# Delta stage of a decoder kernel: values turned token-major as pairs of f16 products instead of f32 transposes

## The chip, the cores and the metric
One core of a Trainium2 chip. The metric is the device time of one execution in microseconds (us): the median of several runs. The engines are TensorE (PE, its weight loads PEld), VectorE (DVE), ScalarE (ACT), GpSimd (POOL) and SyncE (SP), each with an instruction queue of its own that it works in order; semaphores tie them together.

## The reference
Two decoder layers over 8 sequences of 256 tokens with 512 features, a layer norm after every block. The change touches one block, the second layer's attention, a gated delta rule with 16 key heads of 128 and two value heads for each:

```
mixed = silu(causal_conv4(x @ Wqkv.T))        # query, key: 16 x 128 channels; value: 32 x 128
query, key = l2norm(query), l2norm(key)
beta, g = sigmoid(b), -exp(A_log) * softplus(a + dt_bias)
for t:                                         # a state of 128 x 128 per head
    state = state * exp(g_t)
    delta = (v_t - k_t @ state) * beta_t
    state = state + outer(k_t, delta)
    out_t = q_t @ state
out = (rmsnorm(out) * norm_w * silu(x @ Wz.T)) @ Wout.T
```

## The kernel before
The whole decoder is one program of stages, one after the other. The delta stage (function `delta_stage`) takes two thirds of its time. It solves the recurrence in chunks of 128 tokens: for each chunk a triangular system is inverted in seven levels (`level_a`, `level_b` on TensorE, `level_p`, `level_xt` on VectorE, `level_x` on ScalarE), and the rest are matrix products.

The work is cut into 64 units: for each of the 16 key heads four units (`it.u` = 0 to 3) of 512 tokens, that is two sequences of two chunks, with both value heads. The stage is a software pipeline over units: `turns(turn)` calls on each engine the same function once a turn, and in turn n an engine works on parts of the units n+2 (projection, convolution, silu), n+1 (products of keys, inverse), n (answers) and n-1, n-2 (output). `it.has(off)` asks whether there is such a unit; `after(name, k, off)` waits until the k-th signal of that name of unit n+off has come. The order within a turn is written out by hand, at the end of each engine's `turn`, and an engine never leaves it. Work that comes once in four turns (splitting the next key head's weights into an f16 high part, on ScalarE, and a low part, on VectorE) is in the same lists: `next_qkv` when it.u(2) is 3, `next_turns_weights` a turn later, `next_z` another turn later, `next_o` when it.u(-1) is 0.

f32 values meet TensorE as pairs of f16: `high` is ScalarE's cast to f16 and `low` is GpSimd's subtraction, value minus high. So the keys and queries (`products_high`, L1909; `products_low`, L1704) and the decayed products (`split_high`, L1920; `split_low`, L1748).

The values (unit n+2, jobs v0 and v1, one value head each): TensorE's projection goes to a PSUM bank, ScalarE's `conv_tap` writes the first tap into `F[:, 2 + v]` (L1949) and the farthest one into `far[:, v]` (L1955), VectorE's `conv_lag` (L2145) adds two taps from the bank, GpSimd's `conv_far` (L1695) adds `far`, and ScalarE's `silu_job` (L1964) works in place in `F`. In the next turn TensorE's `values_token_major` turns the 8 blocks of 128x128 by f32 transposes (L2565), and ScalarE's `token_major` (L1933) takes them out of PSUM. `far` has two buffers, used by q and v0 and by k and v1.

ScalarE's list around the place of the change, and GpSimd's:

```python
silu_job("v0"); gate(0); products_high(0); products_high(1); split_high(0); split_high(1)
conv_tap("v1"); level_x(1, 1); next_qkv(0); next_qkv(1); split_high(2); split_high(3)
first_answer(1); gate(1); level_x(2, 1); silu_job("v1"); next_qkv(2)
sc.preload_act_table_set("natural_log_exp_and_others"); key_norm(); next_z(0); next_z(1)
decays(0, 2); level_x(3, 1); output_squares(0, 0)          # end of ScalarE's turn
# GpSimd: ... squares_low(1); products_low(0); products_low(1); gm sums; cju copy;
#   conv_far("v1"); split_low(0); V16; split_low(1); low_L(0); split_low(2); low_L(1); split_low(3)
```

`level_x` is L1893. On TensorE `level_a(4)` (L2482) opens the next turn and waits for the third `level_x`; VectorE splits the z weights (`low`, L2083) behind ScalarE's split (L1801), and its `add_out` (L2286) frees the bank that the next projection job takes.

Of the kernel before, what the change touches and what calls it, by code (L numbers as in the profile page):

```python
# [7 lines left out]
F16 = mybir.dt.float16  # L8
BF16 = mybir.dt.bfloat16
ALU = mybir.AluOpType  # L10
ACT = mybir.ActivationFunctionType
# [3 lines left out]
P = 128  # L15
# [1382 lines left out]
def delta_stage(nc, X, consts, WbaT, dtb, alog, Wqkv, Wz, Wout, convw, normw, gt_dram):  # L1398
    with ExitStack() as ctx:
        pt = Parts(nc, "delta", ctx)  # L1400
        sb, counter = pt.sb, pt.counter
        bank = pt.banks()
        ident, ident16 = consts["ident"], consts["ident16"]
# [22 lines left out]
        F = sb("F", [P, 4, 512])  # L1426
# [24 lines left out]
        g = {}  # L1451
        for name, per in dict(
            qj=4, zj=2, wj=4, tap0=4, taps=8, far=4, conv=4, silu=4, sq=2, zsilu=2, wadd=4,
            fh=2, fl=2, sql=2, kss=1, qss=1, ke=1, lnk=1, sk=1, rk2=1, eq=1, gm=4, cju=1, e=8,
            s=3, la=8, dg=2, lt=2, ll=2, vt=2, v=2, v16=1,
            pa=7, px=5, pd=6, pm=7, xc=5, xt=7, xir=1, xti=1,
            sv=7, u0=2, r=2, w=2, t16=1, t2=1, o=2,
            ahi=4, alo=4, so=8, rr=1, lr=1, rn0=1, rn=3, ogs=8, og=2, ct=2, ch=2, cl=2,
        ).items():
            g[name] = counter(name, per)  # L1460
# [51 lines left out]
        def high_half(i):  # L1512

            return sq[:, i, :].bitcast(BF16).rearrange("p (n h) -> p n h", h=2)[:, :, 1]

        def cw_tap(t, k):
            return cw[:, t * 4 + k:t * 4 + k + 1]
# [89 lines left out]
        def _(pool):  # L1607
# [57 lines left out]
            def turn(it):  # L1665
# [24 lines left out]
                def conv_far(job):  # L1690
                    i = QKV[job]
                    after("taps", 2 * i + 2, 2)
                    after("far", i + 1, 2)
                    dst, src = (t.rearrange("p (b t) -> p b t", b=2) for t in (F[:, i, :], far[:, i % 2, :]))
                    gp.tensor_tensor(dst[:, :, 3:256], dst[:, :, 3:256], src[:, :, 0:253], ALU.add)\  # L1695
                        .then_inc(g["conv"].sem, 1)
# [44 lines left out]
                def split_low(n):  # L1741
                    after("ahi", n + 1, 1)
                    if n != 2:
                        after("o", 2, -1)
                    else:
                        after("sv", 4, 0)
                    by_sequencer()
                    gp.tensor_tensor(split_to(n, it.u(1), 1), LA[:, :, split_from[n]:split_from[n] + P],  # L1748
                                     split_to(n, it.u(1), 0), ALU.subtract).then_inc(g["alo"].sem, 1)

                if it.has(2):
                    conv_far("v1")
                if it.has(1):
                    split_low(0)
# [23 lines left out]
                if it.has(1):  # L1778
                    low_L(1)
                    split_low(3)  # L1780

            turns(turn)

        @block.scalar
        def _(act):
# [41 lines left out]
            def turn(it):  # L1827
                def after(name, k, off):
                    if it.has(off):
                        act.wait_ge(g[name].sem, g[name].at(k, it.n(off)))  # L1830
# [72 lines left out]
                def products_high(i):  # L1903

                    if not it.has(2):
                        return
                    after("silu", i + 1, 2)
                    after("s", 3, 1)
                    sc.activation(Fh[:, :, 1 - i, :], by_half(i), ACT.Copy).then_inc(g["fh"].sem, 1)  # L1909
# [27 lines left out]
                def conv_tap(job):  # L1937

                    if not it.has(2):
                        return  # L1940
                    i = QKV[job]
                    after("qj", i + 1, 2)
                    if job == "q":
                        after("s", 3, 1)
                        if it.u(2) == 0:
                            act.wait_ge(w_c.sem, w_c.at(1, it.kh(2)))
                    if job == "v0":
                        after("vt", 2, 1)
                    sc.activation(F[:, i, :], bank[AT[job] % 2][:, :], ACT.Copy, scale=cw_tap(i, 3))\  # L1949
                        .then_inc(g["tap0"].sem, 1)  # L1950
                    if i < 2:
                        after("conv", 3 + i, 1)
                    else:
                        after("conv", i - 1, 2)
                    sc.activation(far[:, i % 2, :], bank[AT[job] % 2][:, :], ACT.Copy, scale=cw_tap(i, 0))\  # L1955
                        .then_inc(g["far"].sem, 1)

                def silu_job(job):

                    if not it.has(2):  # L1960
                        return
                    i = QKV[job]
                    after("conv", i + 1, 2)
                    sc.activation(F[:, i, :], F[:, i, :], ACT.Silu).then_inc(g["silu"].sem, 1)  # L1964
                    if i < 2:
                        after("silu", i + 1, 2)
                        after("kss", 1, 1)
                        after("qss", 1, 1)
                        sc.activation(sq[:, i, :], F[:, i, :], ACT.Square).then_inc(g["sq"].sem, 1)

                def gate(t):

                    if not it.has(0):
                        return
                    after("zj", 1 + t, 0)
                    after("og", 2, -1)
                    sc.activation(flat(gz[:, 2 * t:2 * t + 2, :]), bank[AT[f"z{t}"] % 2][:, :], ACT.Silu, scale=CS)\  # L1977
                        .then_inc(g["zsilu"].sem, 1)
# [10 lines left out]
                def next_qkv(c):  # L1989
                    if it.u(2) == 3 and it.has(2):  # L1990
                        after("qj", 1 + c, 2)
                        high("qkv", c, it.kh(2) + 1)
# [41 lines left out]
                output_high(1)  # L2034
                silu_job("v0")
                gate(0)
                products_high(0)
                products_high(1)
                split_high(0)
# [9 lines left out]
                level_x(2, 1)  # L2049
                silu_job("v1")  # L2050
                next_qkv(2)
                sc.preload_act_table_set("natural_log_exp_and_others")
                key_norm()
                next_z(0)
# [299 lines left out]
        def _(pe):  # L2354
# [42 lines left out]
            def turn(it):  # L2397
                def after(name, k, off):
                    if it.has(off):
                        pe.wait_ge(g[name].sem, g[name].at(k, it.n(off)))  # L2400
# [154 lines left out]
                def values_token_major(b_):  # L2555
                    if not it.has(1):
                        return
                    if b_ == 0:
                        after("silu", 4, 1)
                        after("la", 4, 1)  # L2560
                    else:
                        after("la", 8, 1)
                    for j in range(4):
                        v_, c = j // 2, j % 2
                        last = te.transpose(bank[(2, 6)[b_]][:, j * P:(j + 1) * P],  # L2565
                                            F[:, 2 + v_, b_ * 256 + c * P:b_ * 256 + (c + 1) * P], ident[:, :])
                    last.then_inc(g["vt"].sem, 1)

                def transpose_out(h):
# [284 lines left out]
```

## Time and profile before

| | before |
|---|---|
| median of 3 runs | 3282.03 us (3278.84 to 3283.53) |
| the profiled execution | 3278.3 us |
| its span in the profile | 3276.6 us, 80440 instructions |
| TensorE busy | 2951.4 us (90%) |
| VectorE busy | 2576.6 us (79%) |
| ScalarE busy | 2401.8 us (73%) |
| GpSimd busy | 1950.9 us (60%) |

The profile is of one execution. A timeline row gives start, duration, engine, line and tiles, then how many instructions are merged in the row, and in brackets the idle time of the engine ahead of it and who ended it. Durations of instructions that follow each other on an engine overlap a little, most of all on TensorE: what one costs its queue is the distance between starts. Some records of products can be missing.

### The profile page before, as it was taken

How to read it: one execution, taken by the hardware profiler on the slowest of the kernel's cores; microseconds unless marked ns; L12 is line 12 of the kernel's file. 1: busy time of each engine (PE TensorE's matmuls, PEld its weight loads, DVE VectorE, ACT ScalarE, POOL GpSimd, SP SyncE). 2: the span in 40 equal slices, each digit the busy share in tenths (PEclk: the TensorE clock that was granted, in tenths of full speed). 3: DMA queues.
4: the chain of work that ended last, by engine and by line, in shares of the span. 5: the costliest groups of instructions: out<-in, count | busy, mean ns of one | idle time of the engine just before them, and what ended most of it. 6: DMA issues, size and time to landing. Idle time of an engine off the chain costs nothing. (4 is left out here: it accounts for less than half of the span.)

```text
span 3276.6 us, 80440 instructions
## 1 busy us (share of the span) xinstructions
PE 2951.4 (90%) x29987; PEld 2015.7 (62%) x30006; DVE 2576.6 (79%) x4692; ACT 2401.8 (73%) x6066; POOL 1950.9 (60%) x2266
## 2 busy tenths in 40 slices
PE   7999887736899999999999999999999999997386
PEld 5666555514566666666676666766766667665243
DVE  4555568885788888888888888888888888886796
ACT  4444343435888888888888888888888888886554
POOL 1111166504877777788777787787877878774000
PEclk9999998968999999999999999999999999999699
DMA  5110043401010110101101011010110101100201
GB/s 219 40 33 27 20 146 108 139 10 58 21 34 21 47 34 23 38 21 47 34 21 40 21 46 34 21 41 21 40 41 21 41 21 36 45 21 1 103 1 52
DMA packets 63473, 146.50 MB, mean 45 GB/s; under 512 B 8704, under 2 KB 17536, under 8 KB 59904
## 3 DMA queue, kind: packets, MB, share of 16 engines
q1 hardware_dynamic: 63104, 141.53, 13.8%
q8 instruction: 237, 3.88, 0.5%
q14 instruction: 132, 1.08, 0.1%
HBM read 128.06 MB, written 13.45 MB: 43 GB/s over the span
## 5 line engine op out<-in xcount | busy, mean ns | idle before, releaser
L2153 DVE TENSOR_TENSOR delta_Pb<-delta_bank,delta_lev 128x512 f16<-128x512 f32 x448 | 310.4, 693 | 148.6 <-PE delta_bank L2482 148.6
L2145 DVE SCALAR_TENSOR_TENSOR delta_F<-delta_bank,delta_cw,delta_F 128x510 f32<-128x510 f32 (+1 forms) x512 | 381.5, 745 | 42.8 <-ACT delta_far L1955 28.7
L2456 PE MATMUL delta_bank<-delta_xh,delta_qkvh 128*128 128x512 f16 x1024 | 390.1, 381 | 6.9 <-DVE delta_F L2145 4.5
L2456 PE MATMUL delta_bank<-delta_xl,delta_qkvh 128*128 128x512 f16 x1024 | 389.2, 380 | 0.0
L2456 PE MATMUL delta_bank<-delta_xh,delta_qkvl 128*128 128x512 f16 x1024 | 388.7, 380 | 0.0
L1695 POOL TENSOR_TENSOR delta_F<-delta_F,delta_far 128x506 f32<-128x506 f32 x256 | 278.4, 1088 | 93.4 <-DVE delta_F L2145 93.4
L1675 POOL TENSOR_SCALAR_AFFINE_SELECT delta_LA<-delta_LA 128x512 f32<-128x512 f32 x128 | 81.5, 637 | 376.3 <-DVE delta_LA L2183 355.4
L2170 DVE CAST delta_XT<-delta_bank 128x512 f16<-128x512 f32 x384 | 262.8, 684 | 50.4 <-PE delta_bank L2501 47.3
L2441 PE MATMUL delta_bank<-delta_zh,delta_xh 128*128 128x256 f16 x1024 | 279.3, 273 | 0.6 <-ACT delta_gz L1977 0.6
L2441 PE MATMUL delta_bank<-delta_zh,delta_xl 128*128 128x256 f16 x1024 | 279.2, 273 | 0.0
L2441 PE MATMUL delta_bank<-delta_zl,delta_xh 128*128 128x256 f16 x1024 | 278.9, 272 | 0.0
L383 POOL TENSOR_TENSOR attn_dg<-ident,attn_ri 128x512 f32<-128x512 f32 x64 | 65.4, 1044 | 325.5 <-DVE attn_ri L611 325.5
L1893 ACT ACTIVATE delta_Xi<-delta_bank 128x512 f16<-128x512 f32 x320 | 191.0, 597 | 81.0 <-PE delta_bank L2497 78.8
L1949 ACT ACTIVATE delta_F<-delta_bank,delta_cw 128x512 f32<-128x512 f32 x256 | 174.9, 683 | 100.7 <-PE delta_bank L2456 100.6
L1748 POOL TENSOR_TENSOR delta_Al<-delta_LA,delta_Ah 128x512 f16<-128x512 f32 x192 | 223.5, 1164 | 5.1 <-ACT delta_Ah L1920 5.1
L903 PE MATMUL conv_bank<-conv_kv,conv_T 128*128 128x288 f32 x640 | 172.1, 425 | 40.0 <-POOL conv_kv L854 32.5
L1964 ACT ACTIVATE delta_F<-delta_F 128x512 f32<-128x512 f32 x256 | 162.6, 635 | 61.7 <-POOL delta_F L1695 61.4
L2450 PE MATMUL delta_bank<-delta_oh,delta_ch 128*128 128x512 f16 x512 | 195.1, 381 | 3.2 <-DVE delta_cl L2258 1.5
L2450 PE MATMUL delta_bank<-delta_oh,delta_cl 128*128 128x512 f16 x512 | 194.8, 380 | 0.0
L2450 PE MATMUL delta_bank<-delta_ol,delta_ch 128*128 128x512 f16 x512 | 194.6, 380 | 0.0
L2183 DVE SCALAR_TENSOR_TENSOR delta_LA<-delta_bank,delta_rk,delta_EL 128x512 f32<-128x512 f32 x256 | 179.1, 741 | 7.9 <-ACT delta_EL L1842 7.3
L2456 PEld LDWEIGHTS delta_bank<-delta_xh,delta_qkvh 128*128 128x128 f16 x1024 | 100.3, 98 | 132.4 <-DVE delta_F L2145 37.7
(375 smaller groups left out, 10171.3 us busy)
## 6 DMA issues: line engine op xcount, KB each, us to landing
delta_Gb<-g_rows SPq DMA_DIRECT2D x64, 512.0 KB, 5.3
conv_wf<-in_W SPq DMA_DIRECT2D x72, 256.0 KB, 3.4
delta_st_qkv<-in_Wqkv SPq DMA_DIRECT2D x17, 1024.0 KB, 8.4
conv_T<-filters SPq DMA_DIRECT2D x32, 256.0 KB, 3.4
delta_st_zo<-in_Wz SPq DMA_DIRECT2D x16, 512.0 KB, 8.1
delta_st_zo<-in_Wout SPq DMA_DIRECT2D x16, 512.0 KB, 6.6
conv_ahead_C<-in_ctx_rev SPq DMA_DIRECT2D x1, 6144.0 KB, 27.7
ternary<-conv_spare SPq DMA_DIRECT2D x36, 128.0 KB, 2.8
```

Source lines behind the costliest of these rows:

```text
L903: last = te.matmul(bk[:, 0:PAIRS], T[:, par, (lo - mb) * P:(lo - mb + 1) * P], kv[:, par, mb, :], start=(mb == 0), stop=(mb == lo))
L1695: gp.tensor_tensor(dst[:, :, 3:256], dst[:, :, 3:256], src[:, :, 0:253], ALU.add)\
L1748: gp.tensor_tensor(split_to(n, it.u(1), 1), LA[:, :, split_from[n]:split_from[n] + P], split_to(n, it.u(1), 0), ALU.subtract).then_inc(g[" ...
L1893: sc.activation(left(Xi[:, :, :], lvl), comp(bank[5], lvl), ACT.Copy).then_inc(g["xc"].sem, 1)
L1949: sc.activation(F[:, i, :], bank[AT[job] % 2][:, :], ACT.Copy, scale=cw_tap(i, 3))\
L2145: ve.scalar_tensor_tensor(dst, src, cw_tap(i, 3 - lag), dst, ALU.mult, ALU.add)\
L2153: ve.tensor_tensor(left(Pb[:, lvl, :, :], lvl), comp(bank[5], lvl), bc(lev[:, lvl, :].rearrange("p (n s) -> p n s", s=1 << lvl), 1, 8), AL ...
L2170: ve.tensor_copy(right(XT[:, it.u(off) % 2, :, :], lvl), comp(bank[7], lvl))\
L2183: ve.scalar_tensor_tensor(LA[:, q, L00:L00 + 512].rearrange("p (a i) -> p a i", a=2), bank[(6, 2)[b_]][:, :].rearrange("p (a i) -> p a i", ...
L2441: ins = te.matmul(bk[:, sub * 256:(sub + 1) * 256], xx[:, kc, tok:tok + P], ww[:, kc, :], start=(r == 0), stop=(r == 11))
L2450: ins = te.matmul(bk[:, :], cc[:, blk, :], ww[:, v_, :], start=(m == 0), stop=(m == 5))
L2456: ins = te.matmul(bk[:, :], ww[:, QKV[job], kc, :], xx[:, kc, tok:tok + 512], start=(m == 0), stop=(m == 11))
```

## The change
The silu of v0 and v1 writes to `far` instead of `F`. ScalarE casts the result to f16 (`values_high`) and GpSimd subtracts (`values_low`); the two halves lie in the space of `F[:, 2 + v]`. TensorE turns each block by two f16 products with the f16 identity, high and low, added up in PSUM. New waits: ScalarE's `far` write of the next turn's q and k waits for the subtraction (signal `vl`) instead of the v convolution, and `values_token_major(0)` waits for the second subtraction instead of the silu.

```diff
+            vh=2, vl=2, s=3, la=8, ...
+        def value_half(v_, part):
+            return F[:, 2 + v_, :].bitcast(F16)[:, part * 512:(part + 1) * 512]
 # GpSimd
+                def values_low(v_):
+                    after("vh", v_ + 1, 2)
+                    gp.tensor_tensor(value_half(v_, 1), far[:, v_, :], value_half(v_, 0), ALU.subtract)\
+                        .then_inc(g["vl"].sem, 1)
                 if it.has(2):
+                    values_low(0)
                     conv_far("v1")
...
                     low_L(1)
                     split_low(3)
+                if it.has(2):
+                    values_low(1)
 # ScalarE
                     if i < 2:
-                        after("conv", 3 + i, 1)
+                        after("vl", 1 + i, 1)
...
-                    sc.activation(F[:, i, :], F[:, i, :], ACT.Silu).then_inc(g["silu"].sem, 1)
+                    dst = F[:, i, :] if i < 2 else far[:, i - 2, :]
+                    sc.activation(dst, F[:, i, :], ACT.Silu).then_inc(g["silu"].sem, 1)
...
+                def values_high(v_):
+                    if not it.has(2):
+                        return
+                    after("silu", 3 + v_, 2)
+                    sc.activation(value_half(v_, 0), far[:, v_, :], ACT.Copy).then_inc(g["vh"].sem, 1)
...
                 gate(0)
+                values_high(0)
                 products_high(0)
...
                 silu_job("v1")
                 next_qkv(2)
+                values_high(1)
                 sc.preload_act_table_set("natural_log_exp_and_others")
 # TensorE
                     if b_ == 0:
-                        after("silu", 4, 1)
+                        after("vl", 2, 1)
...
-                        last = te.transpose(bank[(2, 6)[b_]][:, j * P:(j + 1) * P],
-                                            F[:, 2 + v_, b_ * 256 + c * P:b_ * 256 + (c + 1) * P], ident[:, :])
+                        cols = slice(b_ * 256 + c * P, b_ * 256 + (c + 1) * P)
+                        for part in range(2):
+                            last = te.matmul(bank[(2, 6)[b_]][:, j * P:(j + 1) * P], value_half(v_, part)[:, cols],
+                                             ident16[:, :], start=(part == 0), stop=(part == 1))
```

## Rows read from the trace of the kernel before

**Rows 1.** Busy time of the engines in a stretch of the delta stage.
```profile
core 0: us, PE busy (x) PEld busy (x) DVE busy (x) ACT busy (x) POOL busy (x), PEclk, DMA share, GB/s
1500.00:1600.00 100.00, 99.69 (x1144) 68.68 (x1142) 87.08 (x155) 88.18 (x224) 77.77 (x82) 1.00 0.08 23
```

**Rows 2.** Timeline, ScalarE in a plain turn: start, duration, engine, work [idle before].
```profile
1471.97 1.16 ACT L1909 ACTIVATE delta_Fh<-delta_F 128x512 f16<-128x512 f32 x2
...
1475.24 0.60 ACT L1893 ACTIVATE delta_Xi<-delta_bank 128x512 f16<-128x512 f32 x1
...
1478.52 0.60 ACT L1977 ACTIVATE delta_gz<-delta_bank 128x512 f32<-128x512 f32 x1 [0.69 <-PE delta_bank L2441]
...
1479.78 0.62 ACT L1964 ACTIVATE delta_F<-delta_F 128x512 f32<-128x512 f32 x1
1480.42 1.28 ACT L2052 ACT_TABLE_LOAD   x1
...
1483.15 0.39 ACT L1842 ACTIVATE delta_EL<-delta_EL,delta_cju 128x128 f32<-128x128 f32 x1
1483.92 0.60 ACT L1893 ACTIVATE delta_Xi<-delta_bank 128x512 f16<-128x512 f32 x1 [0.38 <-PE delta_bank L2497]
```

**Rows 3.** Timeline, GpSimd in the same plain turn and at the next one's start.
```profile
1472.69 2.28 POOL L1704 TENSOR_TENSOR delta_Fl<-delta_F,delta_Fh 128x512 f16<-128x512 f32 x2 [0.23 <-ACT delta_Fh L1909]
...
1478.55 1.09 POOL L1695 TENSOR_TENSOR delta_F<-delta_F,delta_far 128x506 f32<-128x506 f32 x1
1479.60 1.17 POOL L1748 TENSOR_TENSOR delta_Al<-delta_LA,delta_Ah 128x512 f16<-128x512 f32 x1
...
1494.06 0.64 POOL L1675 TENSOR_SCALAR_AFFINE_SELECT delta_LA<-delta_LA 128x512 f32<-128x512 f32 x1 [6.48 <-DVE delta_LA L2183]
```

**Rows 4.** Timeline, TensorE in the same plain turn.
```profile
1476.56 0.40 PE L2482 MATMUL delta_bank<-delta_Xi,delta_Lt 128*128 128x64 f16 x8
...
1486.16 0.40 PE L2482 MATMUL delta_bank<-delta_Xi,delta_Lt 128*128 128x64 f16 x8
```

**Rows 5.** Timelines of ScalarE, GpSimd and TensorE in a qkv turn.
```profile
1437.78 1.14 ACT L1909 ACTIVATE delta_Fh<-delta_F 128x512 f16<-128x512 f32 x2
...
1447.10 0.63 ACT L1964 ACTIVATE delta_F<-delta_F 128x512 f32<-128x512 f32 x1 [1.72 <-POOL delta_F L1695]
...
1451.29 0.58 ACT L1893 ACTIVATE delta_Xi<-delta_bank 128x512 f16<-128x512 f32 x1
...
1438.74 2.73 POOL L1704 TENSOR_TENSOR delta_Fl<-delta_F,delta_Fh 128x512 f16<-128x512 f32 x2
...
1445.98 1.08 POOL L1695 TENSOR_TENSOR delta_F<-delta_F,delta_far 128x506 f32<-128x506 f32 x1
...
1451.92 0.41 PE L2482 MATMUL delta_bank<-delta_Xi,delta_Lt 128*128 128x64 f16 x8
```

**Rows 6.** Timelines of ScalarE, VectorE and TensorE in a z turn.
```profile
1518.57 0.58 ACT L1893 ACTIVATE delta_Xi<-delta_bank 128x512 f16<-128x512 f32 x1
...
1517.39 2.37 DVE L2083 SCALAR_TENSOR_TENSOR delta_zl<-delta_st_zo,delta_zh 128x512 f16<-128x512 f32 x2
...
1521.47 0.67 DVE L2286 SCALAR_TENSOR_TENSOR X<-delta_bank,X 128x512 f32<-128x512 f32 x1
...
1520.24 0.40 PE L2482 MATMUL delta_bank<-delta_Xi,delta_Lt 128*128 128x64 f16 x8
...
1522.42 0.38 PE L2456 MATMUL delta_bank<-delta_xh,delta_qkvh 128*128 128x512 f16 x1
```

**Rows 7.** Timeline, TensorE: four f16 products, and four f32 transposes.
```profile
1500.77 0.39 PE L2596 MATMUL delta_bank<-delta_V,delta_XT 128*128 128x128 f16 x4
1500.99 1.04 PE L2576 MATMUL delta_bank<-ident,delta_og 128*128 128x128 f32 x8
...
1528.34 0.64 PE L2565 MATMUL delta_bank<-ident,delta_F 128*128 128x128 f32 x4
1528.81 0.38 PE L2456 MATMUL delta_bank<-delta_xl,delta_qkvh 128*128 128x512 f16 x1
```

**Rows 8.** Who waited for L1893 from 850 to 2950 us: us, times.
```profile
  PEld delta_bank L2482: 7.2, 17
```

More of the change, by code:

```diff
@@ L1454, in delta_stage @@
             fh=2, fl=2, sql=2, kss=1, qss=1, ke=1, lnk=1, sk=1, rk2=1, eq=1, gm=4, cju=1, e=8,
-            s=3, la=8, dg=2, lt=2, ll=2, vt=2, v=2, v16=1,
+            vh=2, vl=2, s=3, la=8, dg=2, lt=2, ll=2, vt=2, v=2, v16=1,
             pa=7, px=5, pd=6, pm=7, xc=5, xt=7, xir=1, xti=1,
```

## The prediction
> **What bounds the kernel now.** I read the table of busy time by stretch first. In 100 us of the delta stage TensorE is busy 99.69, ScalarE 88.18, VectorE 87.08 and GpSimd 77.77, at the full granted clock [rows 1]. TensorE's queue is therefore full, and a microsecond that it loses at a wait is a microsecond of the kernel. Then I read the timeline, engine by engine, because shares say nothing of order: every engine works its turn in a written order. The stage has 64 units, one a turn, in groups of four per key head, and the turns of a group differ in the weight splits they carry: one splits next qkv weights (the qkv turn, 16 of them), one the next z weights (the z turn, 15), and two carry nothing in the part that matters (plain turns, 33). One of each kind lies in the rows: plain [rows 2 to 4], qkv [rows 5], z [rows 6]; others of a kind look the same.
>
> The row to keep in mind is ScalarE's cast `level_x(3)` (L1893), which TensorE's `level_a(4)` (L2482) waits for at the start of the next turn. In ScalarE's queue it stands behind `silu_job("v1")`, the Exp table load and four Exp instructions. In the plain turn it starts at 1483.92, ends 0.60 later at 1484.52, and TensorE needs it at 1486.16: 1.64 of slack [rows 2, 4]. In the z turn it ends at 1519.15 for 1520.24: 1.09 [rows 6]. In the qkv turn it ends at 1451.87 and TensorE starts at 1451.92: none [rows 5]. The question is how much later than now this cast comes.
>
> **TensorE's part.** Removed are 8 f32 transposes a turn, added are 16 f16 products. Four transposes run from 1528.34 to the next product's start at 1528.81: 0.47. Four f16 products of 128 columns with weights of their own run from 1500.77 to 1500.99: 0.22, so eight take 0.44 [rows 7]. That gains 0.03 for each of two groups, 0.06 a turn, 64 turns: -4 us. The bounds are 0 and -6 us (0.05 a group, if the rounding of the four starts falls that way). The weight loads lie under the products, so I count nothing for them.
>
> **The two casts on ScalarE.** `values_high` is an f32 to f16 copy of 128x512, as the `Fh` casts are (L1909). Two of those take 1.16 from first start to last end and overlap by a tenth [rows 2], so one occupies 0.53 (bounds 0.52 and 0.58). The first stands ahead of `products_high` and moves the Fh casts, the Ah casts, the v1 taps and `level_x(1)` by 0.53. In the plain turn `level_x(1)` ends at 1475.84 and is needed at 1476.56 [rows 2, 4], so that is covered, and ScalarE's own lateness is gone by its waits for TensorE: one of 0.69 is in the rows [rows 2]. The cast moves GpSimd, though: its `Fl` subtraction waits 0.23 for the first Fh cast, which is the last thing to arrive [rows 2, 3], so GpSimd's whole queue behind it moves by 0.53. The second cast follows `silu_job("v1")`, whose result it reads: it adds 0.53 and a second hand-over from the writer to the reader on one engine. The silu starts at 1479.78 and the table load behind it at 1480.42, 0.64 later [rows 2]; with a dependent cast between, the load comes some 0.67 + 0.64 = 1.31 after the silu, 0.67 more than now.
>
> **The two subtractions on GpSimd.** `values_low` has the form of `split_low` (f16 out, f32 and f16 in, 128x512): 1.16 long, and the queue moves on after 1.12 (bounds 1.10, and 1.37 from the slowest pair of Fl subtractions, 2.73 for two) [rows 3, 5]. The second one stands at the turn's end, in front of a wait of 6.48 for VectorE [rows 3], and its readers (the next turn's k taps and transposes) come microseconds later: nothing. The first one stands in front of `conv_far("v1")` (L1695), and the silu of v1 waits for that. Nothing in GpSimd's queue is idle between the Fh casts and there, so both delays arrive in full.
>
> **The sum by kind of turn.**
> Plain turn: L1695 starts at 1478.55 + 0.53 + 1.12 = 1480.20 and ends 1.09 later at 1481.29 [rows 3]; the silu starts at 1481.33 in place of 1479.78, 1.55 late; with the cast the table load is 1.55 + 0.67 = 2.22 late. The last Exp ended at 1483.54, now 1485.76 [rows 2]; `level_x(3)` starts then and ends at 1486.36, 0.20 past the 1486.16 at which TensorE wants it [rows 4]. Stall 0.20, 33 turns: 7 us.
> z turn: the same 2.22, but two weight splits fill the slack: the cast ends at 1521.37 for 1520.24: stall 1.13 + the hand-over of 0.05. VectorE's split of z (L2083), which runs straight behind ScalarE's, comes about 1.66 late (the first split of z weights ends at 1519.05 instead of before 1517.39) and with it the additions of w results that free the banks of the q job: the one at 1521.47 then ends at 1521.47 + 1.66 + 0.68 = 1523.8, while TensorE wants to begin q at 1522.42 + 1.2 = 1523.6 [rows 6]. I add 0.2 for it. 1.4 a turn, 15 turns: 21 us.
> qkv turn: GpSimd starts Fl directly behind its own work, so the Fh cast, which came at 1437.78 + 0.6 = 1438.4, delays it from 1438.74 to about 1439.0: 0.3 in place of 0.53. The silu is released by L1695, whose end moves from 1447.06 by 0.3 + 1.12 = 1.42 [rows 5]; a split of qkv weights stands between silu and cast, so the cast adds only 0.53: 1.95 late, with no slack. TensorE loses 1.95, 16 turns: 31 us. A first part of it may already be lost at `level_x(1)` in this turn; that is the same lateness and isn't counted twice.
> Together 7 + 21 + 31 - 4 = +55 us. Lateness isn't carried into the next turn: ScalarE waits for TensorE's q product and GpSimd its 6.48. The profiled execution took 3278.3 (span 3276.6) and the median is 3282.0, so 3333 by the one and **3337 us** by the other, which I forecast.
>
> **Bounds.** With the low costs and 0.3 less lateness (a split that hides better than thought), qkv gives 1.65, z 0.9, plain 0: 26 + 14 - 6 = +34. With a subtraction of 1.37 and casts of 0.58, lateness grows by 0.35: 2.3, 1.75 and 0.55 give 37 + 26 + 18 = +81. The likeliest case's own range is 3312 to 3363.
>
> The Trainium skill bears on the high end: its page "GPSIMD Engine Reference", section 1, says that GpSimd's SBUF interfaces are shared with VectorE, with contention for VectorE instructions that have two SBUF inputs. By that rule a subtraction beside one of the weight splits would be longer than 1.12; the pair of 2.73 agrees, though the rows don't show its cause. The sum goes without it.
>
> **Rivals.**
> *Hidden, no change* (6 in 100). GpSimd idles over 6 us a turn and ScalarE over 11 in 100, more than the 2.3 and 1.1 added. If the lateness of `level_x(3)` stayed under the slack, only TensorE's -4 us would be left: 3278. It decides at 1.64 in a plain turn and 1.09 in a z turn, but at 0 in a qkv turn, where TensorE already waits for this cast: TensorE waited 17 times for it, 0.4 each [rows 8]. Those idle times lie behind other points of the queue, which speaks against it.
> *Faster* (4 in 100). If an f32 block cost TensorE four f16 passes, or 0.22, the change would gain 8 x (0.22 - 0.11) = 0.88 a turn, -56 us, and with the low bound of the stalls, +34, the time would be about 3260. Four blocks took 0.47, not 0.88 [rows 7], which speaks against it. The page "FP8 and Floating Point Precision" of the Trainium skill, section TensorE Precision Notes, has this price: true FP32 takes four passes. The trace doesn't agree for these transposes; the page "TensorE: Matmul & The Clock Gate", section Terms, names a transpose mode that is four times faster for FP32, and with that the rule wouldn't apply.
> *A bank chain as well* (6 in 100). VectorE, made late by ScalarE, would free banks late in every kind of turn, 0.3 to 1.0 more a turn: +80 to +120, 3362 to 3402. For it speaks that the q start in the z turn has only 0.27 of slack [rows 6]; against it that VectorE waits for TensorE behind each stall.
> *Half of it* (6 in 100). The plain and z turns absorb all and only the qkv turns pay part: +8 to +30.
>
> **Chances.** The forecast case has 78 in 100, the rivals 6, 4, 6 and 6. A measurement of this kernel can tell about 0.2% (7 us) from no change. Slower by more than that: 78 + 6 + 6 = 90; within it 6; faster 4. The range 3312 to 3363 leaves some 2 in 10 outside.
>
> **What would show it.** In the profile after: L2482 with new waits for ScalarE's L1893, some 50 us in all and longest in the qkv turns; the silu L1964 waiting for GpSimd's L1695 in plain and z turns too; the values' products twice in number with 0.44 for eight; ScalarE and GpSimd busier by about 1.2 and 2.3 a turn and TensorE's share lower. If TensorE's waits stayed at a few microseconds, the slack was misread. If they are at another line (a bank, the `lt` copies), the place was misread. If the eight products take much over or under 0.44, the first term was.

## The result, and the profile after

The changed kernel takes 3362.74 us (median of 4 runs, 3360.73 to 3365.16) against 3280.44 (4 runs, 3277.54 to 3283.53) on the same chip: ratio 1.0252, interval 1.0238 to 1.0265, so 82 us slower. Forecast was 3337, range 3312 to 3363; on the 3282.03 of the forecast the ratio gives 3364.7, just past the high end. The direction and the place were right, the size was not.

Busy time by stretch of the changed kernel, same columns as [rows 1]:

```profile
core 0: us, PE busy (x) PEld busy (x) DVE busy (x) ACT busy (x) POOL busy (x), PEclk, DMA share, GB/s
1500.00:1600.00 100.00, 97.32 (x1118) 65.28 (x1117) 82.42 (x145) 84.33 (x216) 79.53 (x85) 0.98 0.14 39
```

TensorE lost 2.4 of its 99.7, and ScalarE and VectorE are less busy too, although ScalarE has more to do: all of them wait. The table of waits from 850 to 3030 us (engine, tile and line that waited, who was waited for: us in all, times, longest):

```profile
ACT delta_far L1976 <- POOL delta_F L1698: 108.6, 62, 2.8
PEld delta_bank L2503 <- ACT delta_Xi L1904: 77.7, 78, 2.1
PE delta_bank L2503 <- ACT delta_Xi L1904: 44.3, 46, 1.8
POOL delta_Fl L1707 <- ACT delta_Fh L1920: 37.0, 61, 0.8
PEld delta_bank L2471 <- DVE X L2307: 21.4, 23, 1.8
PE delta_bank L2471 <- DVE X L2307: 10.7, 8, 1.4
PE delta_bank L2588 <- DVE delta_LA L2204: 4.5, 16, 0.3
```

The second row answers to [rows 8], where the same wait was 7.2 in 17. `level_a` (now L2503) waits for `level_x` (L1904) 78 times, once or more in nearly every turn. The first row is the cause named in the forecast: the silu of the values waits for GpSimd's `conv_far`, v1's for 1.42 to 1.52 in every plain and z turn and for 2.8 in every qkv turn, where it was 1.7. The rows for L2471 and L2588 are others, not in the forecast.

The distances between the starts of `level_a(0)` give each kind of turn its length over the whole stage:

| turn | before | after | difference | forecast, net of the exchange |
|---|---|---|---|---|
| plain, 30 | 34.08 | 34.25 | +0.17 | +0.14 |
| z, 15 | 34.08, one of 35.75 | 35.50 in 7; 37.26 to 38.45 in 8 | mean +2.47 | +1.34 |
| qkv, 16 | 34.92 | 37.38 | +2.46 | +1.89 |
| the first two | 32.81, 30.71 | 34.00, 33.11 | +3.6 in all | as plain |

30 x 0.17 + 15 x 2.47 + 16 x 2.46 + 3.6 = 5.1 + 37.1 + 39.3 + 3.6 = 85. The two profiled executions lie 86 apart, the medians 82: the loss is in these turns.

The seven intervals from one `level_a` to the next within a turn place it further. In a plain turn the one from `level_a(3)` to `level_a(4)` grew from 5.09 to 5.22, the stall behind `level_x(3)`, and the last one from 4.51 to 4.57.

**The qkv turn.** TensorE and VectorE, timelines of the changed kernel, one after the other:

```profile
1468.07 0.41 PE L2503 MATMUL delta_bank<-delta_Xi,delta_Lt 128*128 128x64 f16 x8 [0.22 <-ACT delta_Xi L1904]
...
1479.70 0.41 PE L2503 MATMUL delta_bank<-delta_Xi,delta_Lt 128*128 128x64 f16 x8 [1.60 <-ACT delta_Xi L1904]
...
1488.25 0.61 PE L2588 MATMUL delta_bank<-ident,delta_F 128*128 128x128 f16 x8 [0.28 <-DVE delta_LA L2204]
```

```profile
1481.35 1.40 DVE L2204 SCALAR_TENSOR_TENSOR delta_LA<-delta_bank,delta_rk,delta_EL 128x512 f32<-128x512 f32 x2
1483.11 0.80 DVE L2233 SCALAR_TENSOR_TENSOR delta_rr<-delta_so,delta_eq 128x4 f32<-128x4 f32 x2 [0.35 <-ACT delta_og L1866]
1483.83 0.68 DVE L2191 CAST delta_XT<-delta_bank 128x512 f16<-128x512 f32 x1
```

The expected stall is the second row: 1.60 ahead of `level_a(4)`. Against the qkv turn of the kernel before, the interval from `level_a(3)` to `level_a(4)` grew from 5.35 to 6.98, by 1.63. The first row is the earlier part, at `level_x(1)`: the interval from `level_a(1)` to `level_a(2)` grew from 5.01 to 5.42, and the next one shrank from 4.79 to 4.65, +0.27 net. The third row is new: the values' products wait for VectorE. The same 4-element operation of VectorE, `rr`, took 0.23 for two in the kernel before in every one of its 64 places (0.22 to 0.25); here it takes 0.80, and 0.73 to 0.81 in 47 of 64 places: all 16 qkv turns, the 30 plain turns, where the last interval's 0.06 is behind it, and one more. What stands beside it is GpSimd's second subtraction:

```profile
1481.54 1.16 POOL L1751 TENSOR_TENSOR delta_Al<-delta_LA,delta_Ah 128x512 f16<-128x512 f32 x1
1482.66 1.16 POOL L1756 TENSOR_TENSOR delta_F<-delta_far,delta_F 128x512 f16<-128x512 f32 x1
1488.34 0.64 POOL L1678 TENSOR_SCALAR_AFFINE_SELECT delta_LA<-delta_LA 128x512 f32<-128x512 f32 x1 [4.52 <-DVE delta_LA L2204]
```

GpSimd then idles 4.52, so the subtraction (L1756) costs its own queue nothing, as forecast. It costs VectorE 0.57, and VectorE's chain is tight in this turn. The last two intervals grew by 0.42 and 0.13.

**The z turn.** VectorE's two splits of the z weights in a short turn (both together, then the first by itself) and in a long one (the same), and GpSimd beside the long one:

```profile
1406.11 2.39 DVE L2104 SCALAR_TENSOR_TENSOR delta_zl<-delta_st_zo,delta_zh 128x512 f16<-128x512 f32 x2 [1.53 <-ACT delta_zh L1812]
1406.11 0.83 DVE L2104 SCALAR_TENSOR_TENSOR delta_zl<-delta_st_zo,delta_zh 128x512 f16<-128x512 f32 x1 [1.53 <-ACT delta_zh L1812]
...
1547.52 2.59 DVE L2104 SCALAR_TENSOR_TENSOR delta_zl<-delta_st_zo,delta_zh 128x512 f16<-128x512 f32 x1 [1.53 <-ACT delta_zh L1812]
1547.52 4.15 DVE L2104 SCALAR_TENSOR_TENSOR delta_zl<-delta_st_zo,delta_zh 128x512 f16<-128x512 f32 x2 [1.53 <-ACT delta_zh L1812]
1551.59 0.68 DVE L2307 SCALAR_TENSOR_TENSOR X<-delta_bank,X 128x512 f32<-128x512 f32 x1
```

```profile
1547.75 1.17 POOL L1751 TENSOR_TENSOR delta_Bl<-delta_LA,delta_Bh 128x512 f16<-128x512 f32 x1
1548.85 0.77 POOL L1785 COPY delta_XT<-ident 128x512 f16<-128x512 f16 x1
1549.53 1.59 POOL L1774 TENSOR_TENSOR delta_Ll<-delta_LA,delta_Lt 128x512 f16<-128x512 f32 x1
1551.09 1.60 POOL L1751 TENSOR_TENSOR delta_Al<-delta_LA,delta_Ah 128x512 f16<-128x512 f32 x1
```

In the short turn the two splits took 2.39 and GpSimd's two operations beside them were the longer ones:

```profile
1406.34 1.61 POOL L1751 TENSOR_TENSOR delta_Bl<-delta_LA,delta_Bh 128x512 f16<-128x512 f32 x1
1407.89 1.23 POOL L1785 COPY delta_XT<-ident 128x512 f16<-128x512 f16 x1
```

The split took 4.13 to 4.15 in 8 of 15 z turns, 2.38 or 2.39 in 7. In the kernel before it took 2.35 to 2.37 [rows 6] in 14 of 15 and 4.23 once, in the turn of 35.75. The second of the two takes 1.64 in short and long turns alike. The difference is in the first: 0.83 or 2.59, and the long one ends 0.49 after GpSimd's copy (L1785) does, in all eight. The late `add_out` (L2307) behind it then holds TensorE's w products:

```profile
1549.92 0.41 PE L2503 MATMUL delta_bank<-delta_Xi,delta_Lt 128*128 128x64 f16 x8 [1.00 <-ACT delta_Xi L1904]
...
1552.33 0.57 PE L2471 MATMUL delta_bank<-delta_oh,delta_ch 128*128 128x512 f16 x1 [1.35 <-DVE X L2307]
...
1696.66 0.39 PE L2471 MATMUL delta_bank<-delta_oh,delta_ch 128*128 128x512 f16 x1 [1.34 <-DVE X L2307]
```

Three of the eight long turns have a third loss. Busy time by stretch behind the two waits of 1.35 and 1.34, and TensorE's timeline in the first stretch:

```profile
1552.00:1556.00 4.00, 3.67 (x17) 1.50 (x18) 3.52 (x8) 1.29 (x9) 1.80 (x2) 0.57 0.00 0
1696.33:1700.33 4.00, 3.35 (x29) 1.67 (x30) 4.00 (x9) 2.28 (x12) 1.80 (x2) 1.00 0.00 0
...
1553.54 0.63 PE L2471 MATMUL delta_bank<-delta_oh,delta_ch 128*128 128x512 f16 x1
1553.97 0.63 PE L2471 MATMUL delta_bank<-delta_oh,delta_cl 128*128 128x512 f16 x1
```

The granted clock is 0.57 in the first and 1.00 in the second: some of the products at 1552 run at the 1.2 GHz level, 0.43 apart in place of 0.215, after TensorE had idled 1.00 and 1.35 within 4 us. Such turns are 38.20 to 38.45 long where the other long ones are 37.26, so it costs 0.9 to 1.2 each, 3.3 us in all.

### The profile page after: what moved, and what is told of

Same layout as the page of the kernel before. It is cut to its first block and busy times, and to the rows that moved or that the text cites. A ratio compares the mean times of both kernels' runs of the same rounds, so it can differ in the third digit from the quotient of the medians.

```text
span 3362.7 us, 81739 instructions
## 1 busy us (share of the span) xinstructions
PE 2967.9 (88%) x30518; PEld 2007.8 (60%) x30518; DVE 2618.6 (78%) x4692; ACT 2467.8 (73%) x6194; POOL 2092.1 (62%) x2394
## 5 line engine op out<-in xcount | busy, mean ns | idle before, releaser
L1904 ACT ACTIVATE delta_Xi<-delta_bank 128x512 f16<-128x512 f32 x320 | 192.2, 601 | 35.5 <-PE delta_bank L2518 35.5
L2471 PE MATMUL delta_bank<-delta_oh,delta_ch 128*128 128x512 f16 x512 | 196.3, 383 | 12.2 <-DVE X L2307 10.7
L2471 PE MATMUL delta_bank<-delta_ol,delta_ch 128*128 128x512 f16 x512 | 196.2, 383 | 0.0
L2471 PE MATMUL delta_bank<-delta_oh,delta_cl 128*128 128x512 f16 x512 | 196.2, 383 | 0.0
L2503 PEld LDWEIGHTS delta_bank<-delta_Xi,delta_Lt 128*128 128x128 f16 x2560 | 112.4, 98 | 136.3 <-ACT delta_Xi L1904 91.3
```

The costliest lines, as they stand in the source:

```text
L1904: sc.activation(left(Xi[:, :, :], lvl), comp(bank[5], lvl), ACT.Copy).then_inc(g["xc"].sem, 1)
L2471: ins = te.matmul(bk[:, :], cc[:, blk, :], ww[:, v_, :], start=(m == 0), stop=(m == 5))
```

## The experiments

Unless said otherwise an edit is against the changed kernel, and a ratio is against the kernel before on the same chip (3277 to 3279 us).

### The products alone

```diff
 # kernel before, TensorE
-  last = te.transpose(bank[...], F[:, 2 + v_, ...], ident[:, :])
+  for part in range(2):
+      last = te.matmul(bank[...], (xh, xl)[part][:, v_, cols], ident16[:, :],
+                       start=(part == 0), stop=(part == 1))
```

The products read fixed f16 tiles that are there anyway; casts and subtractions are absent and the values are not computed.

> The kernel before, with the 8 f32 transposes a turn replaced by 16 f16 products on two fixed f16 tiles; no casts, no subtractions, so the values that enter the recurrence are not the values. Theory (the exchange on TensorE is nearly free, the loss is the late cast level_x(3) and VectorE held up beside GpSimd): -1 to -4 us against before. Rival (the products cost TensorE more than the transposes, and that is part of the 82 us): +10 us or more. Rival (an f32 block costs four passes): -50 us.

Measured: 1.0000 (0.9990 to 1.0009), 3276.32 us. Turns of 34.06 and 34.90 for 34.08 and 34.92: the exchange gains 0.02 a turn, 1.3 us, not 4. So f32 transposes and f16 pairs cost TensorE the same, and the *Faster* rival is excluded.

### The split alone

```diff
-  for part in range(2):
-      last = te.matmul(bank[...], value_half(v_, part)[:, cols], ident16[:, :], ...)
+  last = te.transpose(bank[...], ident[:, :], ident[:, :])
```

Values come out as the identity; everything else of the change stays.

> The changed kernel, with TensorE doing 8 f32 transposes of the identity a turn in place of the 16 products; casts, subtractions and all waits stay. Theory: all of the loss is still there, +80 to +90 us against before. Rival (the products are part of the loss): +70 or less.

Measured: 1.0242 (1.0225 to 1.0259), 3357.52 us. Qkv turns 37.40, plain 34.27. That is 81 us over the kernel before: within the noise the whole loss comes from the split.

### Casts without subtractions, and subtractions without casts

```diff
 # casts only                                   # subtractions only
-  values_low(0) / values_low(1)           |    -  values_high(0) / values_high(1)
-  after("vl", ...)                        |    -  after("vh", v_ + 1, 2)
+  after("vh", ...)                        |    +  after("silu", v_ + 3, 2)
```

With casts only, both products of a block take the high half; with subtractions only, a fixed f16 tile is subtracted, and both products take the result.

> The changed kernel without GpSimd's two subtractions (the low halves are left out; both products read the high half; the waits for the subtraction are waits for the cast). Theory: GpSimd still 0.53 late by the first cast, the table load 0.67 more, 1.2 in all, under the slack of 1.64 in a plain turn, 0.1 over it in a z turn, 0.8 to 0.9 in a qkv turn: +12 to +18 us, and no turns with a long z split. Rival (every added microsecond on ScalarE or GpSimd counts the same): the casts are a third of the added work and cost a third, +27 us.

> The changed kernel without ScalarE's two casts (the high halves are left out; the subtraction takes a fixed f16 tile and both products read its result). Theory: silu of v1 1.12 late, no more: nothing in plain turns, 0 to 0.3 in z turns, 1.1 in qkv turns and 0.55 more there by the second subtraction beside VectorE's rr: +25 to +35 us. With e3 that makes less than the whole 82, because slack is used up only by both together. Rival (costs add up): e3 and e4 together give 82.

| | ratio | us | plain | z | qkv |
|---|---|---|---|---|---|
| casts only | 1.0065 (1.0048 to 1.0082) | 3297.83 | 34.06 | 34.39, one of 36.18 | 35.71 |
| subtractions only | 1.0175 (1.0158 to 1.0192) | 3335.18 | 34.06 | 35.00, 36.76 or 38.1 | 36.05 or 37.07 |

Both cost more than my theory had: +21 for 12 to 18, and +57 for 25 to 35. The order of the two is as expected, and in the plain turn either alone is free, as it should be with a slack of 1.64 for a lateness of 1.1 to 1.2. With casts only the qkv turn is as expected (+0.79 for 0.8 to 0.9) and the excess is in the z turns. With subtractions only it is in both kinds. The z turns of 36.76 and more, 8 of 15, have the long split again (4.81 for two, 3.05 in the others), so subtractions bring it without any cast. The qkv turns of 37.07 are the 12 in which `rr` took 1.25; in the 4 of 36.05 it took 0.24. Parts of 21 and 57 add up to about the whole 82, which by itself would fit "costs simply add"; the kinds of turn show that it is a coincidence of unlike terms: in the plain turns 0 and 0 make 0.17, while the long z turns are as many with the subtractions alone as with both parts.

### The first subtraction behind `conv_far`

```diff
-                    values_low(0)
                     conv_far("v1")
+                    values_low(0)
```

> The changed kernel with the first subtraction moved behind conv_far of v1 in GpSimd's list. Theory (the silu of v1 and the cast level_x(3) behind it are late): silu 0.53 late instead of 1.6, table load 1.2, so the qkv turn as in the run without subtractions (35.7) plus 0.5 for the second subtraction, 36.2; plain turns 34.07; z turns 34.4 or, where VectorE is held up, 36 to 37. In all +30 to +45 us against before. Rival (only the amount of added work counts, not its place): +80.

Measured: 1.0134 (1.0118 to 1.0151), 3324.82 us, 46 over the kernel before: 37 of the 82 us go with the order of two instructions. Qkv turns 36.26, 1.12 less: exactly the step of GpSimd's queue that the forecast had for one subtraction. Short z turns 34.4, also 1.1 less. Long ones (37.25 and 38.4) are still there, 6 of 15, though VectorE's split starts 1.1 less late.

The plain turn is a miss: 34.07 expected, 34.24 measured. The stall behind `level_x(3)` did go (5.22 back to 5.09), but the last interval grew from 4.57 to 4.69. VectorE's and GpSimd's timelines, this kernel:

```profile
1503.24 1.30 DVE L2233 SCALAR_TENSOR_TENSOR delta_rr<-delta_so,delta_eq 128x4 f32<-128x4 f32 x2
1503.27 1.18 POOL L1756 TENSOR_TENSOR delta_F<-delta_far,delta_F 128x512 f16<-128x512 f32 x1
```

`rr` now meets the start of the second subtraction and takes 1.29 to 1.39 in all 30 plain turns, where the changed kernel has 0.73 to 0.76. So the second subtraction costs something in plain turns too, and how much depends on where `rr` meets it.

### The second subtraction made small

```diff
-  gp.tensor_tensor(value_half(v_, 1), far[:, v_, :], value_half(v_, 0), ...)
+  n = 512 if v_ == 0 else 2
+  gp.tensor_tensor(value_half(v_, 1)[:, 0:n], far[:, v_, 0:n], value_half(v_, 0)[:, 0:n], ...)
```

The second value head's products take its high half twice.

> The changed kernel with the second subtraction cut to 2 columns of 512 (its low half is left out, both products of v1 read the high half). Theory (the second subtraction is free for its readers, but VectorE's rr, which has two SBUF inputs, waits behind it in qkv turns and TensorE's values wait for VectorE): qkv turns fall from 37.38 to 36.85, z and plain turns stay, -8 to -10 us against the changed kernel, +72 to +76 against before. Rival (the 0.5 in the qkv turn comes from ScalarE's lateness): no change, +82.

Measured: 1.0232 (1.0215 to 1.0249), 3354.24 us. Qkv turns 36.82 for 36.85 expected, 0.56 below the changed kernel's, and `rr` is back at 0.22 to 0.24 for two in every row. In the plain turns the last interval is back at 4.51. So the operation that I had costed at nothing is worth 0.56 x 16 = 9 us in the qkv turns, through VectorE.

### The z split with one input

```diff
 # VectorE, low("z")
-  ve.scalar_tensor_tensor(chunk(name, c, 2), chunk(name, c, 0), split_scale(name), chunk(name, c, 1), ...)
+  ve.tensor_scalar(chunk(name, c, 2), chunk(name, c, 0), split_scale(name), None, ALU.mult)        # e6
+  ve.tensor_scalar(chunk(name, c, 2), chunk(name, c, 0)[:, 0:1].to_broadcast([P, 512]), ...)       # e9
```

The low part of the z weights is wrong in both; the second reads one column only.

> The changed kernel, with VectorE's low split of the z weights from the second key head on as a scaled copy with one SBUF input (the subtraction of the high part is left out there). Theory (VectorE's work with two SBUF inputs is held up while GpSimd works; that makes the z turns of 37.3 and 38.4): the split falls from 1.2 or 2.1 to 0.7 each, every z turn takes 35.2 to 35.3 (1.17 for level_x(3) alone), the others don't move: -18 to -22 us against the changed kernel, +60 to +65 against before. Rival (the long z turns come from the split's wait for ScalarE): z turns stay between 35.5 and 38.4.

> [...] Theory, mended (VectorE waits for GpSimd's running operation when it needs the second port: with two SBUF inputs, or with one in a fast mode): no z split is over 1.5 for two, every z turn takes 35.2, -14 to -20 us against that run and +60 to +68 against before. Rival (any work of VectorE between SBUF tiles is held up by GpSimd): z turns of 36.8 and 37.9 as in that run, +81.

Measured: 1.0248 (1.0231 to 1.0265), 3362.01 us, and 1.0226 (1.0212 to 1.0241), 3354.97 us. The splits of the second kernel, VectorE's timeline in a long turn:

```profile
1545.90 3.66 DVE L2105 TENSOR_SCALAR delta_zl<-delta_st_zo 128x512 f16<-128x512 f32 x2 [1.53 <-ACT delta_zh L1812]
```

Two took 3.66 or 3.67 in 7 of 15 turns and 1.85 in 8; in the first kernel 3.65 or 3.66 in 9 and 1.85 in 6. I had tied the hold-up first to VectorE instructions with two SBUF inputs, then to a faster mode of one input that the broadcast was meant to prevent. The first form of the theory fell. The second isn't tested by them: the broadcast changed no duration (first split 0.56 or 2.37, second 1.33 or 1.37, in both kernels), and each is 0.2 to 0.3 shorter than with two inputs. In the same traces the feed-forward stage has a one-input operation of VectorE of this size (L1244, 128x512, f32 to a 16-bit type) at 0.43, where an undisturbed split with two inputs takes 0.69. By these times both kernels had the one-input split in its quick form, with and without the broadcast. That it is GpSimd's doing at all was then open.

### GpSimd's work beside the z split made small

```diff
 # GpSimd, z turns only: split_low(2), split_low(3), low_L(0), low_L(1)
-  gp.tensor_tensor(split_to(...), LA[:, :, a:a + P], ...)
+  w = 2 if it.u(0) == 3 and it.has(0) and n > 1 else P
+  gp.tensor_tensor(split_to(...)[:, :, 0:w], LA[:, :, a:a + w], ...)
```

The rest of those low halves keeps old numbers. VectorE's list is untouched.

> The changed kernel, but in the z turns GpSimd's subtractions that stand beside VectorE's z split (low_L(0), low_L(1), split_low(2), split_low(3)) take 2 columns of each block in place of 128; the rest of those tiles keeps old numbers. VectorE's own work is untouched. Theory (each of the two engines holds the other up while both work SBUF to SBUF, and in the long z turns VectorE's second split waits until GpSimd's copy and low_L(1) are through): the two z splits take about 1.6 us (0.79 each, as the single rows show) in all 15 z turns, the products of w no longer wait 1.35 for VectorE, no z turn is above 35.6, and the time falls by 15 to 25 us against the changed kernel, to about 3343; the qkv turns stay at 37.4. Rival (the hold-up is VectorE's own, from its PSUM or from the ScalarE cast that writes the tile next to it): 4.15 in about half of the z turns as before, and the time stays within 5 us of 3363.

Measured: 1.0207 (1.0190 to 1.0224), 3346.09 us (3343 expected). VectorE's and GpSimd's timelines at the same place:

```profile
1543.98 1.30 DVE L2106 SCALAR_TENSOR_TENSOR delta_zl<-delta_st_zo,delta_zh 128x512 f16<-128x512 f32 x2 [1.55 <-ACT delta_zh L1814]
1545.21 0.68 DVE L2309 SCALAR_TENSOR_TENSOR X<-delta_bank,X 128x512 f32<-128x512 f32 x1
```

```profile
1543.11 0.20 POOL L1776 TENSOR_TENSOR delta_Ll<-delta_LA,delta_Lt 128x8 f16<-128x8 f32 x1
1543.28 0.20 POOL L1752 TENSOR_TENSOR delta_Bl<-delta_LA,delta_Bh 128x8 f16<-128x8 f32 x1
1543.43 0.76 POOL L1787 COPY delta_XT<-ident 128x512 f16<-128x512 f16 x1
1544.12 0.62 POOL L1776 TENSOR_TENSOR delta_Ll<-delta_LA,delta_Lt 128x8 f16<-128x8 f32 x1
1544.70 0.65 POOL L1752 TENSOR_TENSOR delta_Al<-delta_LA,delta_Ah 128x8 f16<-128x8 f32 x1
```

The two splits take 1.30 in all 15 turns, 0.69 each, every z turn is 35.24 to 35.36, the qkv turns stay at 37.40 and the weight loads' wait for `add_out` is 7.2 in 16, longest 0.5, where the changed kernel has 21.4 in 23, longest 1.8. VectorE's own code wasn't touched, so the 2.39 as well as the 4.15 are GpSimd's doing. The split is as late as before, and the interval behind it, from `level_a(4)` to `level_a(5)`, is 5.24 where the kernel before has 5.23; in the changed kernel it is 5.50 in short turns, 7.26 in long ones and 8.2 to 8.45 where the clock falls. The expectation had the wrong one of the two waiting: it is the first split, as the rows of the z turn show. It works both ways: here GpSimd's subtraction of 8 elements a partition takes 0.20 alone and 0.62 beside the split. It is worth 17 us by the times, 14 with each time against the kernel before on its own chip, 18 by the spans and 21 by the z turns of the two traces.

### The whole change in another order

```diff
 # GpSimd
+  values_low(1, 1)          # at the head of the next turn, before unit_diagonal(0)
...
-  values_low(0)
   conv_far("v1")
+  values_low(0, 2)
...
-  values_low(1)
 # ScalarE
   sc.preload_act_table(ACT.Silu)
+  values_high(1, 1)         # next turn, before conv_tap("q")
...
-  values_high(0)
   products_high(0)
...
   split_high(3)
+  values_high(0, 2)
...
-  values_high(1)
```

It computes the reference with the same operations in the same number as the changed kernel.

> The whole change in another order: first cast behind split_high(3), where ScalarE waits for TensorE anyway, first subtraction behind conv_far of v1, second cast in the next turn between the Silu table load and the q taps (a wait of 0.9 to 1.7), second subtraction at the head of GpSimd's next turn, ahead of its wait of some 6 us. Theory: no lateness of silu v1 or level_x(3), plain 34.06, qkv 34.9 to 35.0; only GpSimd's 1.1 later end of turn may hold up VectorE's z split in some z turns. -2 to +10 us against before. Rival (work on ScalarE and GpSimd costs wherever it stands): +40 or more.

Measured: 0.9995 (0.9986 to 1.0005), 3277.63 us. Waits for ScalarE's `level_x` and busy time, this kernel:

```profile
PEld delta_bank L2502 <- ACT delta_Xi L1903: 10.7, 22, 1.6
```

```profile
1500.00:1600.00 100.00, 99.82 (x1165) 68.90 (x1163) 87.40 (x155) 91.28 (x229) 84.63 (x87) 1.00 0.08 23
```

TensorE is back at 99.82, with ScalarE 3.1 and GpSimd 6.9 above [rows 1]. Turns are 34.06, 34.07 and 34.90, and the z splits take 2.34 to 2.44 throughout. So the added 2.3 us on GpSimd and 1.1 on ScalarE a turn fit into their idle time; the 82 us are wholly a matter of where they stand. It is no faster than the kernel before.

### The same, with VectorE's qkv splits later

```diff
 # VectorE
-                next_qkv(0)
-                next_qkv(1)
                 residual(1)
                 level_xt(2, 1)
+                next_qkv(0)
...
                 level_xt(3, 1)
+                next_qkv(1)
```

> The reordered change, with VectorE's first two low splits of the next qkv weights moved to later and separate places in its turn. Theory (the 34.9 of the qkv turn, 0.84 over a plain turn, is VectorE late by these two splits at two bank waits of TensorE): qkv turns 34.4 to 34.7, -3 to -7 us against before, beyond both kernels. Rival (the late cast level_x(3) alone makes it): no change against before.

Measured: 1.0075 (1.0063 to 1.0088), 3303.26 us, a miss: slower by 24 us, with qkv turns of 36.02 for 34.90. From the table of waits:

```profile
PEld delta_bank L2470 <- DVE X L2306: 19.9, 17, 2.5
PE delta_bank L2470 <- DVE X L2306: 11.6, 17, 2.0
```

The weight loads' wait was 7.0 in 16 without this edit. The splits now stand where `add_out` frees banks: in the qkv turn the interval from `level_a(3)` to `level_a(4)` grew from 5.35 to 5.87 and the next one from 5.24 to 5.62. One z turn is 36.75 long, with z splits of 5.26. Whether a version exists that beats both kernels stays open.

## Why the prediction was off, step by step

**The bound and the place: right.** The waits of `level_a` for `level_x` grew from 7.2 to 77.7 (PE's own row: 44.3; forecast "some 50"), with 1.6 in each qkv turn and 1.0 in each z turn at `level_a(4)`. The silu waits for GpSimd in every kind of turn, GpSimd's Fl for the first cast (10.0 before, 37.0 after), and moving the first subtraction takes back 1.12 a turn, as the queue step says.

**Plain turn: right in kind, the number partly by luck.** Net forecast 0.14, measured 0.17. The stall behind `level_x(3)` is 0.13 for 0.20; 0.06 at the turn's end comes from the second subtraction beside `rr`, which the forecast had at nothing; and the exchange gives back 0.02, not 0.06.

**z turn, the part through ScalarE: right.** Forecast 1.13 + 0.05; the interval up to `level_a(4)` grew from 5.09 to 6.26, by 1.17. Net, the seven short turns are 1.41 longer for 1.34.

**z turn, VectorE: mis-sized, the largest error.** The step "I add 0.2 for it", worked from a split that is late but keeps its 2.37, fails: the late split takes 4.15 in 8 of 15 turns. That makes 37.26 of 35.50, and 38.20 to 38.45 where the clock falls too: (2.47 - 1.34) x 15 = 17 us over the forecast. The sentence "others of a kind look the same" hid the sign of it: one z turn of the kernel before has a split of 4.23. VectorE's part is 0.26 in a short turn, 2.0 or more in a long one, 1.3 on average where the sum had 0.2. The experiment with small GpSimd work takes all of it away, 14 to 21 us. It is the place of the rival *A bank chain as well*, but not its mechanism: the bank is late because GpSimd holds the split up, in z turns only, and the split's late start alone costs nothing there.

**qkv turn: one term put at nothing.** At `level_x(3)` the stall grew by 1.63, at `level_x(1)` by 0.27 net, together 1.90 for 1.95: the sum of lateness was right. The step "its readers ... come microseconds later: nothing" for the second subtraction fails. It holds for the queue, and not for VectorE, whose `rr` runs beside it: 0.56 x 16 = 9 us. The forecast net was 1.89, measured 2.46.

**The exchange: too large.** 0.06 a turn forecast, 0.02 measured, 2.7 us of 82. The eight products start 0.45 after the values' first, near the 0.44 expected; the four transposes' 0.47 [rows 7] read from one distance hid a rounding as large as the gain.

Together: 55 forecast, 17 in the z turns, 9 in the qkv turns, 1 in the plain turns and 3 in the first two turns, which the sum took as plain ones, make the 85 of the traces; the medians say 82.

**The page set aside.** The page "GPSIMD Engine Reference" of the Trainium skill, section 1, says that GpSimd's SBUF interfaces are shared with VectorE, with contention for VectorE instructions of two SBUF inputs or in a two-port mode. By that rule both missing terms should have been in the sum, and the trace agrees for `rr` and for the z split with two inputs. The z split with one input doesn't speak against it: it was held up too, two took 3.66, but in its quick form, and no run here has a one-input form that is shown to run without a two-port mode. The forecast used the rule for GpSimd's subtractions at the high end alone and not for VectorE's operations. The rows of before already had it: 2.37 for two z splits [rows 6]. In the same trace the first key head's two, with GpSimd idle beside them, took 1.29:

```profile
764.08 1.29 DVE L2083 SCALAR_TENSOR_TENSOR delta_zl<-delta_st_zo,delta_zh 128x512 f16<-128x512 f32 x2
```

**What stays open.** Why the z split is short in one turn and long in the next, with starts relative to GpSimd's that differ by 0.02 us or not at all: in the short case GpSimd's operations are the longer ones, in the long case the split, so one of the engines gives way, but what picks it no run shows. The traces have one hint. Where the split follows other work of VectorE without a pause (the kernel before, the products alone, the two in another order), 2 of 60 are long. Where VectorE had idled 0.4 to 1.6 us for ScalarE's split just before, 50 of 120 are, though only 1 of the 15 with casts only; the experiment with small GpSimd work is not counted. Also open is why the clock fell behind some waits and not behind others: behind 3 of the 8 pairs here, behind 3 of 8 single waits of 2.0 with subtractions only, and behind 4 of 6 of 2.5 with the first subtraction moved.

## What to carry to other kernels

Price an operation moved onto GpSimd twice: once in its own queue, and once for every VectorE operation on SBUF that will run beside it, and after every shift check which ones those are. Ask of each added operation not how long its engine is idle but whose wait ends behind its place; the same instructions cost 82 us in one order and nothing measurable in another. When the trace of the kernel before shows one operation with two durations (2.37 and once 4.23), the longer one is a cost that a small shift can make common.

## What the runs showed of the hardware

- VectorE and GpSimd, both working SBUF to SBUF, hold each other up by whole operations: two 128x512 splits took 1.30 beside small GpSimd work, 2.38 or 4.15 beside 128x512 subtractions, and in the long case the first split ended 0.49 after GpSimd's copy; GpSimd's 0.20 became 0.62, and its 1.16 became 1.6.
- A VectorE operation of 4 elements pays as well: two took 0.73 to 0.81 for 0.23, and 1.30 where they met the subtraction's start.
- A one-input form of the split, with its column broadcast or not, was held up too: 1.85 or 3.66 for two, where one of that size takes 0.43 in a stage without such work beside it.
- An f32 transpose of 128x128 costs TensorE what two f16 products do, to 0.02 us in eight.
- Two TensorE waits of 1.00 and 1.35 within 4 us were followed by products at the 1.2 GHz level for some 3 us, at 0.9 to 1.2 us a turn, in 3 of 8 such turns.
